# Cross-attention block: in the first full pair, VectorE normalises the odd tile ahead of that pair's first two sums

## The reference

```python
Q = (img_embed @ Wq).reshape(B, -1, H, D).transpose(0, 2, 1, 3)
K = (sent_embed @ Wk).reshape(B, -1, H, D).transpose(0, 2, 1, 3)
V = (sent_embed @ Wv).reshape(B, -1, H, D).transpose(0, 2, 1, 3)
score = jnp.einsum('bhqd,bhkd->bhqk', Q, K) / math.sqrt(D)
attn = jax.nn.softmax(jnp.where(mask, score, -jnp.inf), axis=-1)
ctx = jnp.einsum('bhqk,bhkd->bqhd', attn, V).reshape(B, -1, H * D)
out = ctx @ Wo + img_embed
mu = jnp.mean(out, axis=-1, keepdims=True)
var = jnp.var(out, axis=-1, keepdims=True)
return (out - mu) * jax.lax.rsqrt(var + EPS) * gamma + beta
```

## Time and profile before

| | |
|---|---|
| median of 3 runs | 357.52 us (357.38 to 357.65) |
| profiled execution | 357.49 us, of it the span of the profile 355.7 us |
| TensorE matmuls busy | 349.1 us |
| VectorE busy | 269.4 us |
| ScalarE busy | 231.4 us |
| GpSimd busy | 192.9 us |
| first full pair (pair 2) | 142.44 to 157.24 us |

### The profile page before, as it was taken

How to read it: one execution, slowest core, us unless ns; L and a number is a source line. 1 busy time by engine, 2 the same in 40 slices (tenths; PEclk the granted TensorE clock), 3 DMA queues, 4 the chain that set the end, 5 groups by cost and what they waited for, 6 DMA issues and landing times. The chain is left out here.

```text
span 355.7 us, 6790 instructions
## 1 busy us (share of the span) xinstructions
PE 349.1 (98%) x2271; PEld 324.7 (91%) x2271; DVE 269.4 (76%) x501; ACT 231.4 (65%) x780; POOL 192.9 (54%) x208
## 2 busy tenths in 40 slices
PE   8999999999999999999999999999999999999994
PEld 6999999999999999888899889989988998899884
DVE  3289998673921267898798978987987989789895
ACT  2467764144333669887876876877778768768560
POOL 0045650000003858579679688687696796885243
PEclk9999999999999999999999999999999999999999
DMA  8998669775635080042242340541522423413012
GB/s 262 416 420 296 268 223 340 274 257 211 222 136 205 0 270 27 3 178 95 85 152 62 141 151 32 178 136 42 178 88 92 151 66 140 148 37 113 31 47 102
DMA packets 19682, 55.80 MB, mean 157 GB/s; under 512 B 1728, under 2 KB 3264, under 8 KB 17728
## 3 DMA queue, kind: packets, MB, share of 16 engines
q1 hardware_dynamic: 18784, 54.38, 42.3%
q10 hardware_dynamic: 864, 1.00, 0.9%
HBM read 46.98 MB, written 8.39 MB: 156 GB/s over the span
## 5 line engine op out<-in xcount | busy, mean ns | idle before, releaser
L628 PE MATMUL pair<-vw_hi,pt_hi 128*128 128x512 f32 x155 | 62.3, 402 | 0.0
L628 PE MATMUL pair<-vw_hi,pt_lo 128*128 128x512 f32 x155 | 60.9, 393 | 0.0
L628 PE MATMUL pair<-vw_lo,pt_hi 128*128 128x512 f32 x155 | 60.5, 390 | 0.0
L1226 POOL TENSOR_TENSOR out_sb<-centred,beta_sb 128x512 f32<-128x512 f32 x30 | 38.8, 1294 | 27.2 <-ACT centred L820 27.2
L1246 POOL TENSOR_TENSOR x_sum<-xt_in 128x256 f32<-128x256 f32 x16 | 11.9, 745 | 63.0 <-DMA xt_in<-x_tiles 62.8
L775 ACT ACTIVATE prob<-c,neg_max 128x77 f32<-128x77 f32 x128 | 43.9, 346 | 0.0
L1271 POOL TENSOR_TENSOR xo_lo<-x_sum,xo_hi 128x512 fp32r<-128x512 f32 x32 | 41.3, 1295 | 0.5 <-ACT xo_hi L799 0.5
L557 PE MATMUL pair<-a_hi,xo_hi 128*128 128x308 f32 x128 | 40.4, 316 | 0.0
L813 ACT ACTIVATE pt_hi<-pair 128x640 fp32r<-128x640 f32 x32 | 22.5, 704 | 26.8 <-PE pair L615 26.8
L557 PE MATMUL pair<-a_lo,xo_hi 128*128 128x308 f32 x128 | 38.8, 303 | 0.0
L557 PE MATMUL pair<-a_hi,xo_lo 128*128 128x308 f32 x128 | 38.8, 303 | 0.0
(11 more groups left out here) (117 smaller groups left out, 959.0 us busy)
## 6 DMA issues: line engine op xcount, KB each, us to landing
w_out<-wo SPq DMA_DIRECT2D x8, 1024.0 KB, 4.8
xt_in<-x_tiles SPq DMA_DIRECT2D x16, 512.0 KB, 4.1
x_in<-x_rows SPq DMA_DIRECT2D x16, 512.0 KB, 4.9
out<-out_sb SPq DMA_DIRECT2D x31, 256.0 KB, 2.2
w_out<-wq_t SPq DMA_DIRECT2D x7, 1024.0 KB, 6.9
w_proj<-wv SPq DMA_DIRECT2D x8, 768.0 KB, 4.6
w_proj<-wk SPq DMA_DIRECT2D x6, 768.0 KB, 8.7
w_out<-wq_t SPq DMA_DIRECT2D x2, 512.0 KB, 7.5
```

Of the source, the lines that this page charges most:

```text
L628: mm = pe.matmul(ps_out[:, i % 2, 0:s.model], ps[:, j, :], v[:, b, j, :], start=(j == 0 and n == 0), stop=(j == s.key_t - 1 and n == len(p ...
L1226: pool.tensor_tensor(out_sb[i % OUT_RING][:, :], centred[i % 2][:, :], beta_sb[:, :], ALU.add)\
```

## The change

Only VectorE's list is changed, and only for p = 2.

```diff
             for p in range(2, NPAIRS):
                 a = 2 * p
-                combine_first(p)
-                normalise(a - 1)
-                split_pt(a - 2)
                 if p == 2:
+                    normalise(a - 1)
+                    combine_first(p)
+                    split_pt(a - 2)
                     centre(0, ps_out[:, 0, 0:s.model])
+                else:
+                    combine_first(p)
+                    normalise(a - 1)
+                    split_pt(a - 2)
                 residual(a - 3)
                 moments(a - 3)
                 max_c11(p)
```

## The result

The changed kernel took 357.09 us (median of 22 runs, 356.41 to 357.69); the kernel before, run beside it, 357.52 (22 runs, 356.75 to 358.06). The ratio is 0.9986, with a 95% interval of 0.998 to 0.9992: about 0.5 us less, between 0.3 and 0.7. The forecast was 357.16.

The account below looks back on a forecast made before the run. TensorE was taken as the bound (matmuls 98% of the span), waiting for VectorE in pair 2, which held 0.85 us extra. Profiled 357.49 − 0.36 = 357.13; with the median 0.03 above, 357.16 us, range 356.9 to 357.6.

Parts of the forecast that it names:

- The release of the normalising: VectorE, pair 2: tile 3's reciprocal starts 0.02 after the exponentials' last read ends, at 146.18 instead of the sum's 146.55.
- The length of the four and the next one: VectorE, pair 2: from tile 3's reciprocal through product and two sums to tile 2's low part, 1.94 us, before 1.93.
- The first stall: TensorE waiting before tile 3's transposes in pair 2: shrinks from 0.39 to 0.03 us, a gain of 0.36.
- The second stall: TensorE waiting before A22, the pair's last product, for the sum C22: 0.31 us, stays as it is.
- What becomes of it: Later pairs and tail: TensorE stays the bound there, so the 0.36 us is handed on to the end.
- Nothing is left: Rival: normalising isn't released earlier, or an unmoved engine swallows the 0.36; time 357.5 us, chance 0.15.
- The whole 0.85 goes: Rival: A22's stall and small steps vanish too, pair 2 like later ones; 356.67 us; 0.5 to 0.85 gained, chance 0.07.
- VectorE held up by GpSimd: Rival: tile 3's moved product waits for a 1.30 us POOL split, costing 0.94, 358.46 us; slower case, chance 0.04.
- The sums had room: Rival that S3 waits for the first sum: only if over 2.9 us later, it moves 0.58; within slower, 0.04.

Follow-up runs that it names:

- recip_only: Kernel before with, for p = 2, only tile 3's reciprocal moved ahead of the two sums, its product behind them; ratio 0.9993 to the kernel before.
- centre_only: Kernel before with tile 0's centring directly behind tile 0's moments, the four instructions in old order; ratio 0.9991 to the kernel before.
- centre_early: Changed kernel with tile 0's centring also moved directly behind tile 0's moments; 356.67 against 357.43 us for the kernel before, ratio 0.9981.
- swap_all: Kernel before with the odd tile's normalising ahead of the two sums in every pair from 2 on; ratio 0.9992 to the kernel before.
- sums_last: Changed kernel with tile 2's low part also ahead of the two sums for p = 2; ratio 0.9987 to the kernel before.
- fill_behind_again: Changed kernel plus an unread 512-column VectorE zero write between tile 3's normalising and pair 2's first sum, run once more; ratio 1.0002 to kernel before.
- fill_ahead: Changed kernel plus an unread 512-column VectorE zero write directly ahead of tile 3's reciprocal; ratio 0.9979 to the kernel before.
- extra_before: centre_early plus a tiny unread VectorE write (8 columns) ahead of tile 1's residual in pair 2; 356.56 against 357.76 us, ratio 0.9973 to kernel before.

## Why the prediction was right

**The release of the normalising.** Predicted 0.02 behind the exponentials' last read, measured 0.03; and predicted 0.37 ahead of the copy's release. In the changed kernel the idle stretch is 0.59 (predicted 0.6); `recip_only` shows the two releases 0.37 apart in one profile.

**The length of the four and the next one.** Predicted 1.94, measured 1.93. The one neighbourhood that the trace of before didn't show, second sum to low part, was taken as 0.40 and is 0.39. The rule that the prediction quotes from the Trainium skill ("VectorE: DVE Perf Modes", "The DRAIN you can't avoid"), read as the full length of the row (0.48), would have been 0.09 too long. The prediction left out what the same section adds, that a next operation that isn't held starts earlier; the 0.39 agrees with that.

**The first stall.** Predicted to fall from 0.39 to 0.03; the step fell from 0.62 to 0.24, a hundredth from a later pair's.

**The second stall.** Predicted to stay, since VectorE and TensorE arrive earlier alike. The step is 0.43 (0.45 predicted), and C22 starts 3.77 after the low part in both kernels. `centre_only` and `centre_early` show that it is VectorE's lateness with the residual, as argued, and that the centring's place is what makes it.

**What becomes of it.** No later pair takes it up: pairs 3 and 4 last 13.96 and 13.95 as before, and `swap_all` confirms that the new order gains nothing there.

**The size.** 0.36 was forecast for pair 2 and 0.38 came. The medians lie 0.43 apart, and the ratio allows 0.3 to 0.7. It stays below the 0.2% that the prediction took as the limit of what can be measured; with 22 runs of each, the interval excludes no change all the same. That the median came within 0.07 of the forecast is partly luck, as runs of one kernel lie up to 1.3 apart. The window of pair 2 is the test.

**The rivals.** "Nothing is left" falls with pair 2's 14.42 and the interval below 1. "The whole 0.85 goes" needed C22 0.7 earlier; it takes the second edit, and then 0.69 goes. VectorE held up by GpSimd: the product that moved took 0.80 as everywhere else. The sums had room: `sums_last` slides them 0.7 further, and pair 2 takes 14.44 where it took 14.42. (The prediction's limit of 2.9 us is counted from the first sum's new place, so it isn't to be set against the 0.58 that it moves by.)

**Where the working was loose.** It counted the gain at the transposes first and treated A22 as a second, equal arrival. `sums_last` shows that with the centring in the chain A22 alone sets the length: the gain reached the end because C22 came earlier, not because the first stall closed. Here both came earlier by the same amount, so the sum didn't suffer.

## What to carry to other kernels

An in-order engine that sits idle at one wait can be given any work whose own release comes earlier. The gain is the difference of the two releases, or the work that fits in it if that is less, and it is worth something only as far as the engine is late for the one that bounds the kernel. Follow that engine's chain to the last place at which the bound engine meets it: a stall further on may be the one that sets the time, and is closed by taking work out of the chain ahead of it. Where a whole run scatters by more than the gain, compare the window of one turn of the loop.

## What the runs showed that was not expected

VectorE lost 0.25 us at one fixed instruction in pair 6, and TensorE 0.16 to 0.18 with it, in each of the eight profiles with the old number of VectorE instructions ahead of it (pair 6 at 14.11 to 14.13). One more instruction, tried at three places in pair 2, removed it each time (13.95 in `fill_behind_again`, `fill_ahead` and `extra_before`). What the engine does in this stretch, no row shows, so the cause is open.
